# Attention of a two-layer block: the row maxima rotate through four accumulator banks, and their matmuls stand two pairs ahead of the scores, in rounds of two groups

## What is computed

```python
q = q * cos + rotate_half(q) * sin          # q = layernorm(x), k = v = ctx_1024
k = k * cos + rotate_half(k) * sin
scores = jnp.einsum('bqhd,bkhd->bhqk', q, k) * scale + bias[None]
attn = jax.nn.softmax(scores, axis=-1)      # over 256 keys, 16 heads
out = jnp.einsum('bhqk,bkhd->bqhd', attn, v)
x = x + jnp.tanh(g_xattn[1]) * out
```

## Time and profile before

| what | value |
|---|---|
| median of the runs of before | 848.79 us |
| their lowest and highest | 848.14 and 858.55 us |
| the profiled execution's own time | 849.06 us |
| its span in the profile | 847.0 us |
| PE busy | 707.5 us (84%) |
| DVE busy | 695.7 us (82%) |
| ACT busy | 488.6 us (58%) |
| POOL busy | 431.4 us (51%) |

### The profile page before, as it was taken

The page is one execution under the profiler, slowest core; times in us unless marked ns, Lnnn a source line. Parts: engine busy times, 40 slices in busy tenths (PEclk is TensorE's granted clock), DMA queues, the critical chain, the costliest instruction groups (busy, mean ns, idle before and its releaser), DMA issues.

```text
span 847.0 us, 16572 instructions
## 1 busy us (share of the span) xinstructions
PE 707.5 (84%) x5075; PEld 514.2 (61%) x5090; DVE 695.7 (82%) x1230; ACT 488.6 (58%) x955; POOL 431.4 (51%) x331
## 2 busy tenths in 40 slices
PE   2365999999999996889999999999999765777775
PEld 1255888888888885556555665656555433444444
DVE  6866888888888878779888889888888658888985
ACT  3343555555554432357777777777777675556553
POOL 3523665556656655444554445554444425655463
PEclk9987999999999999979999999999999897888999
DMA  8710000000000000010000000000001000000011
GB/s 272 221 43 0 1 1 1 0 0 0 0 0 1 1 2 0 1 51 2 2 3 1 1 1 1 1 1 1 1 1 51 2 1 5 34 25 25 26 38 50
DMA packets 17719, 18.35 MB, mean 22 GB/s; under 512 B 1670, under 2 KB 16912, under 8 KB 17680
## 3 DMA queue, kind: packets, MB, share of 16 engines
q1 hardware_dynamic: 17084, 17.66, 6.5%
q10 hardware_dynamic: 596, 0.20, 0.1%
HBM read 13.39 MB, written 4.19 MB: 21 GB/s over the span
## 4 chain that ended last, share of the span: by engine, by line
PE 51%; DVE 22%; issue 12%; ACT 7%; POOL 5%; DMA 1%; DVEq 1%; POOLq 0%; ACTq 0%; SPq 0%
PE ps_o L528 9%; PE a_ps_t L567 7%; PE a_ps_m L585 6%; DVE maxima L1509 5%; PE a_ps_pv L621 4%; DVE f_ps_small L1594 4%; PE ps_gu L492 4%; PE ps_gu L494 4%; PE ps_gu L493 4%; PE a_ps_s L606 3%; DVE f_hcode L1610 2%; PE a_ps_pv L629 1%; ACT stack_t L920 1%; PE f_ps_h L709 1%; ACT probs L929 1%
## 5 line engine op out<-in xcount | busy, mean ns | idle before, releaser
L1509 DVE TENSOR_REDUCE maxima<-a_ps_m 128x2 f32<-128x512 f32 x256 | 166.1, 685 | 36.5 <-PE a_ps_m L585 35.7
L929 ACT ACTIVATE probs<-a_ps_s 128x512 f32<-128x512 f32 x256 | 149.4, 602 | 43.5 <-PE a_ps_s L606 41.1
L585 PE MATMUL a_ps_m<-stack_t 64*128 64x256 f32 x512 | 109.1, 332 | 19.7 <-DVE maxima L1509 16.7
L585 PEld LDWEIGHTS a_ps_m<-stack_t 64*128 64x128 f32 x512 | 69.5, 192 | 79.3 <-DVE maxima L1509 49.9
L606 PE MATMUL a_ps_s<-stack_t 64*128 64x256 f32 x512 | 100.5, 310 | 4.6 <-ACT probs L929 3.7
L1152 POOL TENSOR_TENSOR stack<-roped,stack 128x512 f32<-128x512 f32 x32 | 42.7, 1335 | 116.2 <-DVE stack L1499 114.7
L528 PE MATMUL ps_o<-w2t,hqt 128*128 128x256 f32 (+1 forms) x384 | 99.6, 394 | 1.2 <-ACT hqt L857 0.7
L492 PE MATMUL ps_gu<-w1h,yth 128*128 128x352 f32 x256 | 86.8, 339 | 4.7 <-DVE h L1322 4.7
L621 PE MATMUL a_ps_pv<-probs,v_aug 128*32 128x256 f32 x1024 | 83.5, 398 | 2.9 <-ACT probs L929 2.7
L920 ACT CAST stack_t<-a_ps_t 128x512 fp32r<-128x512 f32 x128 | 71.0, 588 | 23.5 <-PE a_ps_t L567 22.2
L567 PE MATMUL a_ps_t<-idf,stack 128*128 128x128 f32 x512 | 76.0, 289 | 8.7 <-POOL stack L1152 4.3
(11 more groups left out here) (178 smaller groups left out, 1608.9 us busy)
## 6 DMA issues: line engine op xcount, KB each, us to landing
xres<-in_x SPq DMA_DIRECT2D x16, 256.0 KB, 3.2
ctx<-in_ctx SPq DMA_DIRECT2D x16, 256.0 KB, 4.1
out_x<-f_y SPq DMA_DIRECT2D x16, 256.0 KB, 2.1
w1a_raw<-in_w_gate_up SPq DMA_DIRECT2D x1, 1024.0 KB, 5.9
w_raw<-in_w_fc SPq DMA_DIRECT2D x1, 1024.0 KB, 5.4
w_raw<-in_w_proj SPq DMA_DIRECT2D x1, 1024.0 KB, 4.8
w_raw<-in_w_down SPq DMA_DIRECT2D x1, 704.0 KB, 9.9
stack_t<-neg_max_t SPq DMA_DIRECT2D x32, 8.0 KB
```

The costliest lines, as they stand in the source:

```text
L585: ins = nc.tensor.matmul(a_ps_m[:, half, n, :], a_stack_t[b.par][rows, 0, pair, c * P:(c + 1) * P], a_stack_t[b.par][rows, 1, pair, :], st ...
L929: nc.scalar.activation(a_probs[:, u % 8], a_ps_s[:, u % 2], ACT.Exp).then_inc(a_exp, 1)
L1509: nc.vector.tensor_reduce(a_maxima[:, b.par, c, 4 * quad + half:4 * quad + half + 3:2], a_ps_m[:, half], X, ALU.max).then_inc(a_v_max, 1)
```

## The change

The diff, cut to its core; `LAST_IN_TURN_BANKS` is 6.

```diff
+        def max_bank(m):
+            pair, half = m // 2, m % 2
+            if pair >= 2 and pair % 2 == 0:
+                return a_ps_t[:, half, :].rearrange("p (a t) -> p a t", t=T)
+            return a_ps_m[:, half]
+
+        def group_in_same_max_bank(m):
+            return m - 4 if m >= 6 else m - 2
...
                 if g >= 2:
                     pe.wait_ge(a_t, b.count(TG, g - 1))
                 elif b.shifted(-1):
-                    pe.wait_ge(a_t, b.shifted(-1).count(TG, TG + g - 1))
+                    pe.wait_ge(a_v_max, b.shifted(-1).count(MU, 2 * LAST_IN_TURN_BANKS + g + 1))
...
-                if m >= 2:
-                    pe.wait_ge(a_v_max, b.count(MU, m - 1))
+                if m in (4, 5):
+                    pe.wait_ge(a_t, b.count(TG, TG + m - 5))
+                elif m >= 2:
+                    pe.wait_ge(a_v_max, b.count(MU, group_in_same_max_bank(m) + 1))
...
             def at_body(b):
                 nxt = b.shifted(1)
                 if not nxt:
+                    at_turn_max(b)
                     pe.wait_ge(a_mt, B)
...
                         at_turn(nxt, g)
+                        if g == 1:
+                            at_turn_max(b)
...
+                if nxt:
+                    for m in range(4):
+                        at_scores_for_max(nxt, m)
+                    for g in range(PG - 1):
+                        at_scores(b, 2 * g + 2)
+                        at_scores(b, 2 * g + 3)
+                        at_times_v(b, g)
+                        if 2 * g + 5 < MU:
+                            at_scores_for_max(nxt, 2 * g + 4)
+                            at_scores_for_max(nxt, 2 * g + 5)
+                    at_times_v(b, PG - 1)
+                    return
                 for m in range(MU):
-                    if nxt:
-                        at_scores_for_max(nxt, m)
...
                 at_times_v(b, PG - 1)
-                if nxt:
-                    at_turn_max(nxt)
...
             def at_body(b):
                 nxt = b.shifted(1)
                 if nxt:
-                    for g in range(6):
+                    at_turned(nxt, 0)
+                    at_max_out(b)
+                    for g in range(1, 6):
                         at_turned(nxt, g)
...
                 at_pv_out(b, 3)
-                if nxt:
-                    at_max_out(nxt)
```

More of the change, by code:

```diff
@@ L143 @@
 PG = 8
+LAST_IN_TURN_BANKS = 6
 def build_main(nc, load, loaded, out_v, g_xattn, g_ffn, w_gate_up, w_down, w_fc, b_fc, w_proj, b_proj, ident, decay,
@@ L584, in at_scores_for_max @@
                     pair = 2 * quad + n
-                    ins = nc.tensor.matmul(a_ps_m[:, half, n, :], a_stack_t[b.par][rows, 0, pair, c * P:(c + 1) * P],
+                    ins = nc.tensor.matmul(max_bank(m)[:, n, :], a_stack_t[b.par][rows, 0, pair, c * P:(c + 1) * P],
                                            a_stack_t[b.par][rows, 1, pair, :], start=True, stop=True)
@@ L657, in at_body @@
                             at_times_v(b, (u - 4) // 2)
-                    if not nxt and m == 8:
+                    if m == 8:
                         turn_w34(2)
                         turn_w34(3)
-                    if not nxt and m == 12:
+                    if m == 12:
                         ff_turn_input(lead[0])
[L663 to L667, removed]
+                pe.wait_ge(a_w34, 4)
+                pe.wait_ge(bias_placed, 48)
+                ff_fc(lead[0], 0)
+                ff_fc(lead[0], 1)
                 at_times_v(b, PG - 1)
-                if nxt:
-                    at_turn_max(nxt)
             def ff_turn_input(b):
@@ L770, in _ @@
                 at_scores_for_max(first, m)
-            at_turn_max(first)
             pe.wait_ge(v_out, B)
@@ L1047, in _ @@
                 l0_hidden_out(last, g)
-            at_max_out(first)
             over_batches(act, at_body)
@@ L1508, in at_row_max @@
                     dve.wait_ge(a_t_mt, b.shifted(-2).count(1, 1))
-                nc.vector.tensor_reduce(a_maxima[:, b.par, c, 4 * quad + half:4 * quad + half + 3:2], a_ps_m[:, half], X,
+                nc.vector.tensor_reduce(a_maxima[:, b.par, c, 4 * quad + half:4 * quad + half + 3:2], max_bank(m), X,
                                         ALU.max).then_inc(a_v_max, 1)
```

## The result

The changed kernel takes 860.46 us in the median (857.93 to 865.49, 18 runs) beside 850.21 us of the kernel before: a ratio of 1.0119 (95% interval 1.0099 to 1.014). It is 1.2% slower, and the interval lies clear of 1. Its profiled execution took 859.52 us with a span of 857.4 us, 10.4 more than before, and no instruction is new: VectorE is busy 693.3 us (before 695.7), ScalarE 486.4 (488.6). TensorE is busy 714.6 us (707.5), at a mean granted clock of 0.936 (0.952).

What follows compares the result with a forecast made beforehand. It took the chain through one body (19.6 us) as the bound, with VectorE 89% busy. Bodies 0 to 13 at +1.0 each give +14.0, the ends -2.0 and -1.5: +10.5, so 859.5 us, range 854 to 865 (845 to 869 with rivals).

Steps and rivals of the forecast that it cites:

- the ends: First batch's maxima and bodies 14 and 15: -2.0 us at the start, -1.5 in body 14, body 15 keeps its order.
- Four maxima ahead: Start of a body: M2 and M3 wait for reductions R0 and R1 with scores S2 queued behind them, +1.6 us a body.
- The negation behind the first copy: Among the transposes: the later negation of the maxima delays the second copy and so M0, +0.3 us a body.
- The end of the body: From V7 to the next transposes: the maxima's transposition leaves this place, 0.80 us shrinks to 0.57, -0.2 us a body.
- The rounds: S2 to V7, seven rounds of S, S, V, M, M: maxima groups from M4 on never wait, 11.4 us against 12.0, -0.6.
- The ring: Two banks of scores and exponentials: a round's second score waits for the previous round's last exponential, 1.58 us against TensorE's 1.29.
- The sum of a body: One body's four terms, 1.6 + 0.3 - 0.2 - 0.6 = +1.1 us, taken as +1.0 because overlaps were rounded up.
- ScalarE's idle time before E2: Sign in the profile: ScalarE would stand idle about 1.5 us before exponential E2.
- no maxima group from M4 on waits for VectorE: Sign in the profile: only M2 and M3 would wait for reductions, 0.5 to 0.9 us each.
- A: Rival: reductions fed without gaps, VectorE's row decides; 831.5 us, or 815 with all 2.2 us a body; chance 0.12.
- B: Rival: the scores' late start is made up in the rounds, body 0 to 0.5 us longer, 845.5 to 852.5 us; chance 0.2.
- C: Rival: the new stop slows TensorE's clock in most bodies, 12 times 1.1 us on top, 873 us; chance 0.13.

Runs made afterwards that it cites:

- early_banks: Changed kernel, same order, but maxima groups M2 and M3 use the transposes' banks, so they wait for transpose copies, not reductions R0 and R1: 841.17 us, ratio 0.9869.
- late_pair: Changed kernel with only maxima groups M2 and M3 moved, behind the first S2, S3, V0; from M4 on unchanged: 840.27 us, ratio 0.9881.
- two_ahead: Changed kernel with only M0 and M1 ahead of S2 and each later maxima pair one round back, same banks: 836.65 us, 0.9825 of the kernel before.
- max_at_end: Changed kernel with the maxima's transposition back behind V7 and their negation back at the end of ScalarE's body: 864.4 us, ratio 1.0129.
- banks_alone: Kernel before in its own order, with only the four banks for the maxima and their waits: 835.23 us, ratio 0.9816.
- order_alone: Changed kernel with its order but only the two old banks for the maxima: 890.32 us, ratio 1.0454.
- spread: Changed kernel with rounds S, M, S, V, M in place of S, S, V, M, M, same banks and four groups ahead: 857.93 us, ratio 1.008.
- two_early: Changed kernel with two maxima groups ahead of S2 and the second pair in the transposes' banks: 831.28 us, ratio 0.9768.
- two_early_spread: Kernel two_early with the rounds S, M, S, V, M as well: 822.24 us, ratio 0.9661.

## Why the prediction was right, point by point

**The total** was forecast at 859.5 us and 1.2% slower; it is 860.46 us and 1.2% slower. The way and the cause were right; that the sum fits so closely is in part luck, as the ends below show.

**Four maxima ahead, +1.6 a body:** measured +1.68 (2.02 less 0.34). It is shown, not only argued: early_banks takes the wait away at the same order, late_pair and two_ahead take M2 and M3 from ahead of S2, and all three get the gain.

**The negation behind the first copy, +0.3:** the transposes grew from 6.17 to 6.49 us, +0.32, and max_at_end brings them to 6.13. S0 starts 4.46 us after the first transposes (before 4.14), where I had +4.4 from the DMAs. I had called that a tie, and it is one: between 406 and 652 us the scores waited for the row of maxima six times in twelve bodies, 1.1 us in all.

**The end of the body, -0.2:** V7 to the transposes fell to 0.59 us as worked out, but from a mean of 0.96 (I had read 0.80 in one body), so it gave 0.37. The bodies alternate between about 0.79 and 1.14 us there, and I had looked at a short one.

**The rounds, -0.6, to 11.4 us from S2 to V7:** 11.33 us, from 12.07, so -0.74. The number was about right and the reason half wrong. I credited the new rounds with it. But banks_alone, in the old order, needs 11.08: the banks give 1.0 us, and S, S, V, M, M takes 0.25 of it back. And order_alone, with the new order on the old banks, needs 12.02, which is no gain over 12.07. The ring that I named is real (spread takes 0.56 us off it), and I take it for the price of the new rounds. The rounds ran on average at (547.64 less 538.10) / 6 = 1.59 us, I had 1.58.

**The sum of a body** was +1.1, rounded to +1.0; at the full clock it is +0.89.

**The ends, and the luck in the total.** From one transposed maxima to the next, bodies 0 to 13 took 12.45 us more than before (from 364.73 to 652.88 us, before from 366.32 to 642.02), where I had +14.0: bodies 1 to 13 gave +13.06, of which about 1.4 is two bodies with a slower clock against one, and body 0 was 0.6 us shorter (20.49 against 21.10). The first transposed maxima stand at 364.7 us in place of 366.3, -1.6 (I had -2.0). Body 14 takes 21.84 us in place of 23.14, -1.3 (I had -1.5). From there to the end it is +0.9, which I had at nothing: body 15 is about 2.5 us longer, with a granted clock of 0.78 in the changed kernel and 1.00 in the one before, and a wait of 1.82 us for the row of maxima in place of 0.67, and what follows it is 1.6 us shorter. These add up to 12.45 - 1.6 - 1.3 + 0.9 = +10.5 us, which is my figure with other terms.

**What the profile was to show.** ScalarE's idle time before E2 is 1.98 us, where I had 1.5. Before M2 TensorE's row was idle for 0.86 us, as forecast; before M3 it shows no such gap where I had put 0.5 to 0.9, since M2's own matmuls fill part of the 0.6 us between the two. The six rounds of the body shown above took from 1.38 to 1.88 us each, a wider spread than the 1.4 to 1.65 of the forecast. I had also written that no maxima group from M4 on waits for VectorE. The waits in TensorE's rows, 406 to 652 us (total us, times, longest), say:

```profile
PEld a_ps_m L599 <- DVE maxima L1532: 29.0, 54, 1.1
...
PE a_ps_m L599 <- DVE maxima L1532: 10.4, 12, 0.9
```

The matmuls wait 12 times, once a body, which is M2. The weight loads (PEld) wait 54 times, M6 and later among them. Those cost nothing: each pair M, M from M4 on starts 0.57 us behind its value group (539.24 less 538.67, 540.85 less 540.28), as it does unhindered.

**The rivals.** A (a gain) saw that there was something to win and had the wrong place for it: with S2 no longer behind the waits on R0 and R1, late_pair, two_ahead and early_banks gain 1.2 to 1.8%. The four banks alone are worth 1.8% (banks_alone); the order made around them lost that and 1.2% more. The Trainium skill (Perfetto Trace Analysis, section Matmuls) says that independent groups of matmuls should rotate through different banks. The ratio of 0.9816 of banks_alone agrees with that. B did not come true: the stop was not covered, and the body is 0.89 us longer, beyond B's 0.5. C came true in two bodies, 1 and 2, which were 1.1 to 1.2 us longer than their like, not in most.

One step I did not take: I never sized the banks and the order apart. And when I did, ahead of banks_alone, my 0.3 us was too small. I had read VectorE's 89% as a wall, but before the change its own waits were 1.8 us a body, and the banks made the body 0.72 us shorter.

## What to carry to other kernels

A lead built into an in-order queue is worth only what stands in banks of its own: every group issued ahead that reuses a bank puts its wait in front of all that follows, and the first rounds are where it shows. Look at what stands behind the first reused bank, and put independent work there (late_pair), or give those groups the free banks (early_banks). And when a change has two parts, size each alone: here the banks gave 1.8%, and the order on top of them took 3.1% (1.0119 over 0.9816).

## What the runs showed of the hardware that I had not expected

Slower clocks went together with a stop of the kind made here. Of the twelve bodies counted in the table, none had a slower clock in the six kernels with 0.34 or 0.80 us from M0 to S2 (two_ahead, late_pair, early_banks, banks_alone, two_early, two_early_spread), and one in the kernel before (0.34 us). With 1.45 us it was three, and with about 2.0 us two, three, five and eight. In the spread kernel a stretch at 1.2 GHz lasted 3.4 us and its body was about 1.0 us longer; in order_alone one lasted 17 us, and the two bodies that it touched were together 5.2 us longer than two at the full clock.

That explains most of where order_alone lies. Its eight slower bodies are together 18.3 us longer than eight of 21.0 us, where the two of the changed kernel lost 2.3. The 16 us between them are most of the 20 us by which it missed the 870 that I expected.

That kernels with the same stop differ (two bodies in the changed one, five in spread) is not explained by the length of the stop. What else decides it stays open, and so does whether the stop itself brings the slower clock: no run here was made for it, the counts come from one profiled execution each, and the mean clock over all executions does not tell two_ahead (0.930 to 0.943) from the changed kernel (0.928 to 0.948).
